# An attention and mixture-of-experts layer: the output bias of batch 0 moved ahead of its query projection, and two steps reordered on GpSimd and on ScalarE

## The reference

```python
x = x + attn(layernorm(x))
x = x + ffn(layernorm(x))
# attn
q, k, v = x@Wq.T + bq, x@Wk.T + bk, x@Wv.T + bv
kv_sum  = cumsum((elu(k) + 1) * v, axis=1)
context = (elu(q) + 1) * kv_sum * SCALE
return context @ Wo.T + bo
# ffn, per token
logits = x @ router_w            # 8 experts, top 2, softmax over the two
routed = sum_k score_k * (silu(x@w1g[e_k]) * (x@w1u[e_k])) @ w2[e_k]
shared = (silu(x@w_gate) * (x@w_up)) @ w_down      # inner width 1024
```

## Time and profile before

| what | value |
|---|---|
| median of 3 runs | 354.12 us (354.0 to 354.18) |
| profiled execution, its own time | 353.77 us |
| its span, first to last instruction | 351.8 us |
| PE busy | 340.8 us (97% of the span) |
| DVE busy | 235.0 us (67%) |
| ACT busy | 214.0 us (61%) |
| POOL busy | 193.4 us (55%) |
| mean granted TensorE clock | 0.997 of full |

### The profile page before, as it was taken

How to read it: one execution, slowest core, us unless ns; L and a number is a source line. 1 busy time by engine, 2 the same in 40 slices (tenths; PEclk the granted TensorE clock), 3 DMA queues, 4 the chain that set the end, 5 groups by cost and what they waited for, 6 DMA issues and landing times.

```text
span 351.8 us, 9162 instructions
## 1 busy us (share of the span) xinstructions
PE 340.8 (97%) x2937; PEld 256.8 (73%) x2937; DVE 235.0 (67%) x585; ACT 214.0 (61%) x389; POOL 193.4 (55%) x282
## 2 busy tenths in 40 slices
PE   7999989999999999999999999999999999999993
PEld 6878868888888898888988465656655566666662
DVE  4989889899899887878788554453544533334441
ACT  3679948797887987746536444445544445544551
POOL 4768986785885868265056444353443535443335
PEclk9999999999999999999999999999999999999998
DMA  6992042576974546835775449559496675875740
GB/s 198 382 347 48 18 111 50 133 142 190 183 212 91 146 160 144 218 89 148 251 236 133 100 80 107 88 90 95 78 117 79 99 108 79 105 101 91 95 69 10
DMA packets 76108, 45.90 MB, mean 130 GB/s; under 512 B 59936, under 2 KB 71200, under 8 KB 75680
## 3 DMA queue, kind: packets, MB, share of 16 engines
q1 hardware_dynamic: 62000, 34.82, 40.8%
q0 software_dynamic: 9392, 10.44, 19.3%
q10 hardware_dynamic: 4672, 0.07, 1.3%
HBM read 19.09 MB, written 12.97 MB: 91 GB/s over the span
## 4 chain that ended last, share of the span: by engine, by line
PE 83%; DVE 7%; POOL 2%; DMA 2%; issue 2%; SPq 1%; ACT 1%; POOLq 0%; DVEq 0%; ACTq 0%
PE bU L1099 13%; PE bG L1099 13%; PE bD L974 9%; PE bU L239 9%; PE bG L239 8%; PE bQ L1124 6%; PE bV L1124 6%; PE bV L239 4%; PE bK L239 3%; PE bK L1079 2%; PE bQ L239 2%; PE bT L974 2%; PE bT L843 1%; PE bT L864 1%; DVE ws_l L1663 1%
## 5 line engine op out<-in xcount | busy, mean ns | idle before, releaser
L1601 DVE SCALAR_TENSOR_TENSOR ab<-bU,sg 128x512 f32<-128x512 f32 x64 | 44.2, 690 | 65.9 <-PE bU L1099 47.5
L774 POOL DMA_INDIRECT out_y<-xs,dst_row x32 | 49.7, 1552 | 61.2 <-DVE dst_row L1938 29.0
L1253 ACT ACTIVATE sg<-bG 128x512 f32<-128x512 f32 x64 | 38.0, 593 | 44.1 <-PE bG L1099 26.9
L1099 PE MATMUL bG<-we,work 128*128 (+1 forms) x216 | 52.6, 380 | 0.0
L1099 PE MATMUL bU<-we,work 128*128 (+1 forms) x216 | 52.6, 379 | 0.0
L572 POOL DMA_INDIRECT x_rows<-rows,slot_u x32 | 41.6, 1301 | 18.2 <-issue 10.7
L1418 ACT ACTIVATE ws_h<-ab 128x512 f16<-128x512 f32 x36 | 22.7, 629 | 41.5 <-DVE ab L1601 37.6
L1923 DVE TENSOR_TENSOR ws_h<-ab,ws_h 128x512 f16<-128x512 f32 x36 | 25.0, 693 | 20.8 <-ACT ws_h L1418 19.7
L1260 ACT ACTIVATE ah<-ab 128x512 f16<-128x512 f32 x32 | 20.1, 628 | 28.9 <-DVE ab L1601 23.9
L1099 PEld LDWEIGHTS bG<-we,work 128*128 128x128 f16 (+1 forms) x216 | 20.7, 99 | 19.3 <-issue 1.6
L1099 PEld LDWEIGHTS bU<-we,work 128*128 128x128 f16 (+1 forms) x216 | 19.8, 99 | 17.4
(11 more groups left out here) (338 smaller groups left out, 816.1 us busy)
## 6 DMA issues: line engine op xcount, KB each, us to landing
stage<-in_w_expert SPq DMA_DIRECT2D x24, 512.0 KB
we<-in_w_shared SPq DMA_DIRECT2D x3, 1024.0 KB, 11.4
out_y<-xs SPq DMA_DIRECT2D x8, 256.0 KB
xs<-bo POOLq DMA_DIRECT2D x7, 256.0 KB, 4.5
xs<-in_x SPq DMA_DIRECT2D x1, 1280.0 KB, 16.6
x_rows<-we SPq DMA_DIRECT2D x9, 134.0 KB
xs<-in_x SPq DMA_DIRECT2D x3, 256.0 KB, 3.7
work<-x_rows SPq DMA_TRANSPOSE x40
```

The source lines that it names most:

```text
L774: pool.indirect_dma_start(out_rows, bass.IndirectOffsetOnAxis(ap=dst_row[:, b:b + 1], axis=0), ya[b % NY], None, bounds_check=NT * P - 1, ...
L1099: ins = pe.matmul(dst[t * n:(t + 1) * n, :], x2[:, hi * KC + k, t * n:(t + 1) * n], w[t][lo][:, k, half, :], start=s == 0 and k == 0, stop ...
L1253: act.activation(sg[q][:], src[:], ACT.Silu, scale=1.0 / WS).then_inc(S["sg_done"], 1)
L1601: dve.scalar_tensor_tensor(out=ab[q][:], in0=src[:], scalar=1.0 / WS, in1=sg[q][:], op0=ALU.mult, op1=ALU.mult).then_inc(S["a_done"], 1)
```

## The change

Four edits, all in the order of work or in the choice of a bank:

1. `add_bo_first` moves from behind batch 1's projections to where `warm(7)` stood, ahead of batch 0's query projection; `warm(7)` and `warm(4)` go. As bank bT is still being read there, the bias goes into bR, and so does the whole output projection of batch 0 (`out_bank(0)`), which `residual(0)` then reads from bR.
2. In exchange the turned rows of batch 2 go into bT instead of bR, with a wait for `l1_done` of batch 1.
3. POOL does `pow2(1)` ahead of `norm1(3)`.
4. ACT does `shared_hi(2, 1)` behind `silu(2, 0)`, `normed1(3)` and `row_hi1(3)` instead of ahead of them.

```diff
         def turn_bank(i):
-            return bR if i == 2 else bT
+            return bT
+
+        def out_bank(i):
+            return bR if i == 0 else bT
...
             slot_constants(1)
+            pow2(1)
             norm1(3)
-            pow2(1)
             gaps(0)
...
                 pe.wait_ge(S["xn1"], TB * (i + 1))
-                if i == 1:
-                    pe.wait_ge(S["l1_done"], 1)
+                if i >= 1:
+                    pe.wait_ge(S["l1_done"], i)
...
                 pe.wait_ge(S["cs_row"], 1)
-                pe.wait_ge(S["l1_done"], 2)
                 for t in range(TB):
-                    pe.matmul(bT[:, t * D:(t + 1) * D], cs_row, bo[0:1, :], start=t == 0, stop=False, skip_group_check=True)
+                    pe.matmul(out_bank(0)[:, t * D:(t + 1) * D], cs_row, bo[0:1, :], start=t == 0, stop=False, skip_group_check=True)
...
-                        ins = pe.matmul(bT[:, t * D:(t + 1) * D], cx[:, k, t * P:(t + 1) * P], w[:, k, :],
+                        ins = pe.matmul(out_bank(i)[:, t * D:(t + 1) * D], cx[:, k, t * P:(t + 1) * P], w[:, k, :],
...
             turn_first(1)
-            warm(7)
+            add_bo_first()
             project(0, "q")
             project(1)
-            add_bo_first()
-            warm(4)
             attend_whole(0)
...
             choice(0)
-            shared_hi(2, 1)
             silu(2, 0)
             normed1(3)
             row_hi1(3)
+            shared_hi(2, 1)
             act_hi(0, 2)
...
-                dve.scalar_tensor_tensor(out=xs_of(i), in0=bT[:].rearrange("p (t d) -> p t d", t=TB),
+                dve.scalar_tensor_tensor(out=xs_of(i), in0=out_bank(i)[:].rearrange("p (t d) -> p t d", t=TB),
```

## The result

The changed kernel takes **356.81 us** in the median (4 executions, 355.62 to 357.40), the kernel before 354.15 us in its executions on the same chip (354.0 to 354.19): ratio 1.0072, interval 1.0041 to 1.0102, so **slower**, by 0.7%. The forecast was 355.5 us with a range up to 356.3: right in its sign, too small, and outside its range. The other three took up to 1.8 us more again, for which there are no rows.

The account below looks back on a forecast made before the run. TensorE, busy 97%, was taken as the bound, with batch 2's power on POOL almost without slack; gains of 1.3 us were spent waiting, gates 1.4 us later: 353.77 + 1.4 = 355.2 profiled, 355.5 us median, range 352.6 to 356.3.

Parts of the forecast that it names:

- Bias matmuls: Batch 0's attention on TensorE: with the bias pass moved ahead, the output projection starts 0.96 us earlier, bounds 0.8 and 1.0.
- The cover: Before batch 0's output projection: TensorE's 0.2 us delay stays hidden ahead of the context at 18.59, with 0.1 us to spare.
- DVE's and ACT's side: Batch 3's first rows: DVE keeps 1.3 us, low half at 41.6, TensorE's keys of batch 3 start 1.3 us earlier.
- POOL's side: POOL from batch 1's power: all behind starts 0.8 us later, wide constants wait beneath DVE's run, first row write at 48.65.
- the deciding question: POOL's two 64-column constants under DVE's run: do they pass between DVE instructions (row writes 46.0) or wait (48.65)?.
- From the row write to the gates: First row write to gate matmuls: gaps(1) done at 55.75, batch 2's power 56.85, gate matmuls 1.4 us later than before.
- the sum: To the kernel's end: 353.77 + 1.4 = 355.2 us for the profiled execution, 355.5 us in the median.
- Rival A: POOL's wide constants each pass behind one DVE instruction, row writes at 46.0; median 352.9 us, faster; chance 0.33.
- my price: POOL's two 64-column constants wait nearly to the end of DVE's run at 48.0, putting the first row write at 48.65.
- Rival B: POOL's wide constants need two DVE instructions each, row writes at 47.7; median 354.6 us; chance 0.20 with the mixtures.
- Rival C: Batch 0's bias part fails: bo lands late or TensorE's clock falls without warming matmuls; some tenths more; chance 0.02.

Follow-up runs that it names:

- after_c: The changed kernel with only the register that holds back a scatter loaded with asserted bounds; 356.41 us, ratio 1.0075 to the kernel before.
- bias_alone: The changed kernel without its steps on POOL and ACT, leaving only the bias matmuls and the banks; 353.23 us, ratio 0.9978 to the kernel before.
- hold_rows: The changed kernel with POOL's last twelve constants at its list's end and batch 0's row writes held until batch 3's transposes landed; 355.29 us, ratio 1.0049.
- const_end: The changed kernel with all twelve constants of the last group moved to the end of POOL's list; 354.25 us, ratio 1.0006 to the kernel before.
- pool_undone: The changed kernel with POOL's list as before, batch 3's first norm ahead of batch 1's power; 353.53 us, ratio 0.9991 to the kernel before.
- act_alone: The kernel before with only ACT's step, shared_hi(2, 1) behind batch 3's first rows; 354.30 us, ratio 1.0006.
- five_late: The changed kernel with the last five constants (L624 to L628) moved to the end of POOL's list; 353.32 us, ratio 0.9976 to the kernel before.
- the controls: The kernel before and the changed kernel, each with only a bounded load of the scatter's hold register; 353.78 us (0.9998) and 356.41 us (1.0075).

## Why the prediction was right in sign and too small

**Bias matmuls, 0.96 us earlier.** Measured 0.71 for the output projection. The cover held; the context itself was 0.16 us late behind an ACT wait for a DMA, and the first matmul came 0.15 us behind it, not 0.06. Size off, and without consequence.

**DVE's and ACT's side, keys of batch 3 1.3 us earlier.** Held: low half at 41.78 (said 41.6), run from 43.91 (43.7), keys at 47.49 (47.4).

**POOL's side, the first row write at 48.65.** Measured 48.67, and yet this step failed: the number came out by compensation. I let every constant but the last two pass as before, "0.8 us later", so that the two 64-column ones would begin at 43.85 and wait to the run's end. They began at 46.82 and passed within 0.95 and 0.74 us, each 0.33 us after the end of one DVE instruction. The first of them came 3.8 us later than before (43.05), and that went into the small ones: 0.86 by the later start and 2.9 net within them. L612 (2.36 against 0.32), L613, L623, L624 and L626 cost 5.2 us more than before, those between them 2.3 us less. What I had called the deciding question, whether wide instructions pass, was not the one that decided. In its place: the small ones, each beside a DVE run without a pause. The rows for the right one stood in the trace: L609 and L610 ran at 36.59 in 0.3 us each because DVE paused for batch 1's power until 36.48 and then did only four steps of 0.2 us. The change removed that pause and ACT's 0.57 us one, and I booked both as gains of DVE alone.

```profile
36.59 0.32 POOL L609 TENSOR_SCALAR slot_w<-mix_at,slot_w 128x4 f32<-128x4 f32 x1
```

**From the row write to the gates, +1.4 us.** Held: power done at 56.77 (56.85), ACT at 57.60 (57.66), gates at 59.89 (59.9). Up to here the sum is right to a few hundredths.

**The sum ended there, and that is why it was too small.** I took the time behind the gates for unchanged. Measured behind it: 0.45 us in front of batch 2's routing in the profiled execution, and 0.44 us more at batch 3's routing in that of `after_c` (85.30 us). The first alone takes the 355.2 forecast for the profiled execution to 355.65; it took 355.62. The remaining 1.2 us up to the median of 356.81 lie in executions without rows: the profiled one was the fastest of four. Their clocks are on record. The two with 0.997 and 0.998 took 355.62 and 356.25 us, both within the forecast's 354.9 to 356.3; the two with 0.993 and 0.994 took 357.36 and 357.40. The sum had no term for the clock, although it foresaw a TensorE stall of 2.7 us; that is the second term put at nothing, worth 0.9 us between the two groups of the nine executions. Why the clock was lower in five of them stays open. `after_c`, from 356.18 to 357.05 us, puts the loss at 2.5 us.

**Rival A and the rule.** The Trainium skill, SBUF — State Buffer, section "Who interferes with whom", gives the shared port to whoever issues first, for its whole instruction; read as the prediction read it, a waiting GpSimd instruction passes at the end of one DVE instruction. In this trace L623, L624, L626, L627 and L628 did so, the 64-column ones too, against my price. L612 did not: it lasted across two of 1.2 us; nor did L613 (39.80, 1.22 us), which ended at 41.02, after both of the shorter DVE instructions that it met. What the exceptions share is not their width: L612, L613 and the 64-column row of 1.51 us in the kernel before are all TENSOR_SCALARs that take a scalar per partition from a tile. No TENSOR_TENSOR among the constants was passed over in any trace here. As L627 and L628 have that form too and passed, it is not enough by itself; it was not tested. Rival A's time was wrong all the same, since by that rule too each of nine constants pays for a DVE instruction once DVE has no pause, and I applied it to the last two alone. **Rival B** had the same fault. **Rival C**: the load of bo was in time. The clock did fall in two of the four executions, to 0.993 and 0.994, and I had given that 0.02. Its reason, the missing warming matmuls, is not borne out: `bias_alone` lacks them as well, and none of its twelve executions was under 0.995.

The loss is an interaction. POOL's step starts the constants 0.86 us later and beneath two weight parts, ACT's step removes the pause in which they would catch up; either one alone is free. Together, here with the bias matmuls, they make batch 2's power late by 1.46 us, and TensorE, 1.2 us ahead, stalls for 2.44 us.

## What to carry over

Before you close a pause on one engine, look at what another engine does in it: in DVE's idle 0.9 us six of POOL's constants passed, and a pause of 1.25 us put back was worth 2.3 us. Price a chain of small instructions beside a busy DVE one by one, each by the DVE instruction it would meet, and not only the wide ones; those of DVE that read a PSUM bank did not hold POOL here. Follow the sum past the point where the loss arises, to the end of the kernel, and look at the clock of every execution before calling a spread noise. Try the parts of a change singly and in pairs; here the bias matmuls alone, or the whole with five constants moved, give 0.2% that the whole change throws away.

## What was not expected of the hardware

- A POOL instruction on 128x4 elements (0.32 us alone) took 2.36 us beside two DVE weight conversions of 1.2 us, 0.1 us longer than both; it took 2.36 or 2.37 us in all ten kernels that have POOL's step.
- POOL's indirect row writes lengthened DMA transposes issued by SP beside them: from issue to TensorE's use 3.83 us with the row writes held back (`hold_rows`) and 4.79 us with them in front (`const_end`). Where they followed 0.3 us behind the transposes it was 4.32 (`pool_undone`) and 4.41 us (`act_alone`).
- A row write behind a wait for a signal started 0.97 us after the last constant (`five_late`) and 0.90 us after TensorE's first use of the transposes waited for (`hold_rows`); behind constants without such a wait it was 0.18 us. In `const_end` it was 0.79 us, and the profile names no wait.
- POOL instructions of 0.2 us kept that time beside DVE instructions that read a PSUM bank (L620 beside L1558), while those beside DVE instructions with two SBUF inputs waited (L623 beside L1663, 1.24 us).
- In nine executions of the whole change, with and without the edit of the controls, the five with a mean granted clock of 0.990 to 0.994 were the five longest, by 0.9 us in the mean, while in `hold_rows` the longest two of twelve had 0.998.
